# Ternary weights of the first block: ScalarE writes the group scale, VectorE decides by a bf16 difference and makes the first weights' low parts, with new turns and PSUM places for the whole program

## The reference

```python
def ternary_quant(w_fp32, g=64):
    w = w_fp32.astype(jnp.bfloat16)
    w_g = w.reshape(-1, g)
    scale = jnp.clip(jnp.mean(jnp.abs(w_g), axis=-1, keepdims=True), 1e-08, None)
    q = jnp.clip(jnp.round(w_g / scale), -1, 1)
    return w + stop_gradient((q * scale).reshape(w.shape) - w)

gate, up = jnp.split(x @ ternary_quant(w_gate_up).T, 2, axis=-1)
h = jax.nn.silu(gate) * up
out = rms_norm(h) @ ternary_quant(w_proj).T

xn = layernorm(x)                       # block 0, attention
q, k, v = xn @ Wq + bq, xn @ Wk + bk, xn @ Wv + bv
```

## Time and profile before

| | |
|---|---|
| median of 3 runs | 1232.33 us |
| span of the profiled execution | 1229.5 us |
| the profiled execution's own time | not given beside its span; the median of the runs lies 2.8 us above the span |
| PE busy | 1096.5 us, 89% of the span |
| DVE busy | 864.2 us, 70% |
| ACT busy | 631.2 us, 51% |
| POOL busy | 503.0 us, 41% |

### The profile page before, as it was taken

How to read it: one execution, slowest core, us unless ns; L and a number is a source line. 1 busy time by engine, 2 the same in 40 slices (tenths; PEclk the granted TensorE clock), 3 DMA queues, 4 the chain that set the end, 5 groups by cost and what they waited for, 6 DMA issues and landing times.

```text
span 1229.5 us, 17428 instructions
## 1 busy us (share of the span) xinstructions
PE 1096.5 (89%) x6541; PEld 718.4 (58%) x6556; DVE 864.2 (70%) x1612; ACT 631.2 (51%) x963; POOL 503.0 (41%) x551
## 2 busy tenths in 40 slices
PE   4579999999999998999389999998789998996998
PEld 2356686765665564675268898987234543553445
DVE  6988767678658999856667326368776779668751
ACT  4445656475568875643235224252176276455473
POOL 5655748466514544413764214053331321141131
PEclk9769999999999999999689999999699999998999
DMA  5905335443260000267350000008626316317220
GB/s 178 291 10 156 81 96 161 126 123 107 49 207 35 35 35 9 82 206 243 94 52 26 1 1 1 1 26 201 156 51 155 108 45 165 92 49 173 71 72 18
DMA packets 86115, 116.42 MB, mean 95 GB/s; under 512 B 29616, under 2 KB 43280, under 8 KB 85264
## 3 DMA queue, kind: packets, MB, share of 16 engines
q1 hardware_dynamic: 47792, 70.28, 19.1%
q0 software_dynamic: 38240, 45.03, 14.7%
HBM read 81.54 MB, written 40.40 MB: 99 GB/s over the span
## 4 chain that ended last, share of the span: by engine, by line
PE 64%; DVE 21%; ACT 5%; issue 4%; POOL 3%; DMA 2%; another core or an unknown queue 0%; SPq 0%; ACTq 0%; DVEq 0%; POOLq 0%
PE pair L691 22%; PE bank L691 19%; PE bank L770 7%; PE pair L760 5%; PE pair L749 5%; DVE max L1152 4%; ACT probs L1670 2%; POOL gathered L2082 1%; PE pair L710 1%; PE bank L778 1%; DVE hidden L1208 1%; DVE hidden L1206 1%; DVE tern_mask L1049 1%; PE pair L790 1%; DVE mix_h L1540 1%
## 5 line engine op out<-in xcount | busy, mean ns | idle before, releaser
L1152 DVE TENSOR_REDUCE max<-pair 128x2 f32<-128x1024 f32 (+3 forms) x256 | 252.6, 1020 | 64.1 <-PE pair L749 36.6
L1670 ACT ACTIVATE probs<-pair 128x1024 f32<-128x1024 f32 (+3 forms) x256 | 213.4, 865 | 112.9 <-PE pair L760 106.4
L749 PE MATMUL pair<-ks,qs 64*128 64x512 f32 (+3 forms) x512 | 111.7, 457 | 28.7 <-DVE max L1152 13.9
L770 PE MATMUL bank<-probs,v 128*32 128x512 f32 (+3 forms) x1024 | 119.0, 542 | 2.0 <-ACT probs L1670 1.3
L760 PE MATMUL pair<-qs,ks 64*128 64x512 f32 (+3 forms) x512 | 103.8, 437 | 13.7 <-DVE max L1152 4.9
L2003 POOL TENSOR_TENSOR h_low<-hidden,h_high 128x512 fp32r<-128x512 f32 x64 | 83.3, 1307 | 77.4 <-ACT h_high L1708 77.0
L749 PEld LDWEIGHTS pair<-ks,qs 64*128 64x128 f32 x512 | 50.8, 198 | 89.2 <-DVE max L1152 35.1
L760 PEld LDWEIGHTS pair<-qs,ks 64*128 64x128 f32 x512 | 46.5, 190 | 81.2 <-ACT probs L1670 25.9
L2100 POOL TENSOR_TENSOR h<-mix_h,h 128x512 bf16<-128x512 f32 x48 | 54.8, 1169 | 75.4 <-DMA h<-comb 49.7
L1702 ACT ACTIVATE hidden<-pair 128x512 f32<-128x512 f32 x64 | 38.0, 597 | 86.5 <-PE pair L691 72.6
L2047 POOL TENSOR_SCALAR_AFFINE_SELECT probs<-probs 128x256 f32<-128x256 f32 x128 | 51.3, 411 | 65.0 <-ACT probs L1670 63.8
(11 more groups left out here) (327 smaller groups left out, 2678.5 us busy)
## 6 DMA issues: line engine op xcount, KB each, us to landing
kept<-q_high SPq DMA_DIRECT2D x64, 256.0 KB, 3.7
qs<-kept POOLq DMA_DIRECT2D x32, 512.0 KB, 4.2
ks<-kept POOLq DMA_DIRECT2D x32, 512.0 KB, 5.2
kept<-q_low SPq DMA_DIRECT2D x32, 256.0 KB, 4.1
expert_in<-in_experts_in SPq DMA_DIRECT2D x16, 352.0 KB, 4.3
expert_out<-in_experts_out SPq DMA_DIRECT2D x16, 256.0 KB, 5.5
h<-comb SPq DMA_DIRECT2D x4, 1024.0 KB, 5.4
x<-in_x SPq DMA_DIRECT2D x4, 512.0 KB, 5.1
```

Of the source, the lines that this page charges most:

```text
L749: made = mm(to[:, hh, 0:n], m.qs[k][slot][r0:r0 + STACK, p, qt * P:(qt + 1) * P], m.ks[k][slot][r0:r0 + STACK, p, 0:n], start=True, stop=k ...
L770: made = mm(to[32 * j:32 * j + 32, q0:T], m.v[b % 2][:, kt, G * g + j, :], m.probs[(2 * kt + j // 2) % 4][:, j % 2, q0:T], start=kt == 0, ...
L1152: V.tensor_reduce(m.max[:, g % 2, :, p, qt], to[:, :, 0:n], AX.X, ALU.max).then_inc(*s.done("top"))
L1670: A.activation(m.probs[(2 * kt + p) % 4][:, :, q0:T], to[:, :, q0:T], ACT.Exp, scale=0.25).then_inc(*s.done("exp"))
```

## The change

- `tern_mean(j)`, a new part on ScalarE, reads the sum from PSUM and writes the scale as bf16. It frees the PSUM place, which `tern_scaled` freed before.
- `tern_scaled(j)` has four instructions in place of five, and none reads PSUM: scale minus magnitude (with the lower bound of 1e-8), the comparison of that difference with the magnitude, magnitude plus difference, and the product.
- `split_first` on VectorE makes the low parts of block 0's Wq, Wk and Wv. `split_low(0)` on GpSimd goes.
- `headed` waits for the `headed` two places earlier, on its own engine.
- Turns (DUE) of all engines and PSUM places (TAKEN) are new.

```diff
@@ DUE (one line of some 150)
-    "tern_sum": "0 2 3 4 7 9 8 10 17 15 16 26",
+    "tern_sum": "0 1 3 4 6 9 8 10 17 13 16 27",
...
@@ FREED
-    "tern_sum": lambda j: [("tern_scaled", (j,))],
+    "tern_sum": lambda j: [("tern_mean", (j,))],
@@ qk and vals, TensorE
-        pe.wait_ge(*at("split_low", k // 3))
+        pe.wait_ge(*(at("split_low", 1) if k else at("split_first")))
@@ VectorE
+    def split_first():
+        dve.wait_ge(*at("split_high", 0))
+        V.tensor_tensor(m.wqk_low[0][:, :, :], m.wqk[0][:, :, :], m.wqk_high[0][:, :, :].bitcast(F32), ALU.subtract).then_inc(*dve.up())
+        V.tensor_tensor(m.wv_low[0][:, :, :], m.wv[0][:, :, :], m.wv_high[0][:, :, :].bitcast(F32), ALU.subtract).then_inc(*s.done("split_first"))
     def tern_scaled(j):
-        t, to = m.tern[j % 3], bank("tern_sum", j)
-        dve.wait_ge(*at("tern_sum", j))
-        V.tensor_scalar(t["scale"][:, :], to[:, 0, :], 1.0 / 64, 1e-8, ALU.mult, ALU.max).then_inc(*dve.up())
+        t = m.tern[j % 3]
+        dve.wait_ge(*at("tern_mean", j))
+        V.scalar_tensor_tensor(t["scale"][:, :], t["scale"][:, :], 1e-8, t["mag"][:, :], ALU.max, ALU.subtract).then_inc(*dve.up())
         dve.wait_ge(*dve.own())
         if j >= 3:
             dve.wait_ge(*at("tern_out", j - 3))
-        V.scalar_tensor_tensor(t["mask"][:, :], t["scale"][:, :], 257.0 / 512, t["mag"][:, :], ALU.mult, ALU.is_lt).then_inc(*dve.up())
-        dve.wait_ge(*dve.own())
-        V.tensor_tensor(t["mask"][:, :], t["mask"][:, :], t["scale"][:, :], ALU.mult).then_inc(*dve.up())
-        dve.wait_ge(*dve.own())
-        V.tensor_tensor(t["scale"][:, :], t["mask"][:, :], t["mag"][:, :], ALU.subtract).then_inc(*dve.up())
-        dve.wait_ge(*dve.own())
-        V.tensor_tensor(t["mask"][:, :], t["mag"][:, :], t["scale"][:, :], ALU.add).then_inc(*s.done("tern_scaled"))
+        V.tensor_tensor(t["mask"][:, :], t["scale"][:, :], t["mag"][:, :], ALU.is_lt).then_inc(*dve.up())
+        V.tensor_tensor(t["scale"][:, :], t["mag"][:, :], t["scale"][:, :], ALU.add).then_inc(*dve.up())
+        dve.wait_ge(*dve.own())
+        V.tensor_tensor(t["mask"][:, :], t["mask"][:, :], t["scale"][:, :], ALU.mult).then_inc(*s.done("tern_scaled"))
@@ headed, VectorE
+        if 4 * b + g >= 2:
+            dve.wait_ge(*at("headed", k, *((b, g - 2) if g >= 2 else (b - 1, g + 2))))
@@ ScalarE
+    def tern_mean(j):
+        act.wait_ge(*at("tern_sum", j))
+        A.activation(m.tern[j % 3]["scale"][:, :], bank("tern_sum", j)[:, 0, :], ACT.Abs, scale=1.0 / 64).then_inc(*s.done("tern_mean"))
```

More of the change, by code:

```diff
@@ L70 @@
     "DVE": {
-        "set_dve": [(0,)], "tern_scaled": keys(range(12)),
+        "set_dve": [(0,)], "split_first": [()], "tern_scaled": keys(range(12)),
         "stat": keys(ALL, B, range(TT)), "cut_low": keys((0, 2, 3), B),
@@ L86 @@
     "ACT": {
-        "tern_cast": keys(range(12)), "norm": keys(ALL, B, range(TT)), "turned": keys(ALL, B),
+        "tern_cast": keys(range(12)), "tern_mean": keys(range(12)), "norm": keys(ALL, B, range(TT)), "turned": keys(ALL, B),
         "biased": keys(B, PAIRS), "q_high": keys(HEADS, B, PAIRS), "exp": keys(HEADS, B, range(G), range(TT), PAIRS), "summed": keys(HEADS, B, range(G)),
@@ L98 @@
     "POOL": {
-        "cast0": [()], "split_low": keys(range(3)), "bring": keys(HEADS, B, range(G)), "max_bring": keys(HEADS, B, range(G)), "tern_out": keys(range(12)),
+        "cast0": [()], "split_low": keys((1, 2)), "bring": keys(HEADS, B, range(G)), "max_bring": keys(HEADS, B, range(G)), "tern_out": keys(range(12)),
         "root": keys(ALL, B), "based": keys(HEADS, B), "with_xn": keys(B),
@@ L326 @@
-    "weigh": "77776666666666666666666677776666666677777777777766666666666666667777666666666666777766667777666677776666777777777777777777776666",
-    "back": "77677667666677777776767676766677",
-    "rows": "402004020442",
-    "out": "76677767666776767676766776667667",
-    "unit": "2402020420004202220202044042044220422040024204202044200424402044",
-    "down": "77767677",
-    "mean": "6777",
-    "proj": "0044022402200440",
-    "gate": "7766667776676776",
-    "gamma": "4024",
-    "inflow_turn": "0202",
@@ new lines @@
+    "weigh": "77776666666666666666777777777777666677776666777766667777666666667777666666666666666666667777777777776666777777777777666666667777",
+    "back": "67666676676677767776766676767667",
+    "rows": "442004044420",
+    "out": "67767767776776767666676776666676",
+    "unit": "2402020420004202400242044002244204422040040240242204424044422244",
+    "down": "77766677",
+    "mean": "7766",
+    "proj": "0444020402200440",
+    "gate": "6667667776776776",
+    "gamma": "4024",
+    "inflow_turn": "2202",
@@ new lines @@
+    "mem_turn": "77776666",
+    "shared": "0202440220420442",
+    "count": "7666",
+    "logit_turn": "7776",
+    "merge": "67",
+    "expert_turn": "6767776777766677",
+    "expert_in": "4224242042400224",
+    "expert_fold": "7767766666766766",
+    "expert_out": "6667766677777667",
+    "spline": "204024022040",
+    "qk2": "2440",
+    "v2": "76766776",
+    "score2": "6776677677767676",
+    "probs_turn": "7676677767667776",
+    "comb_turn": "6766",
+    "mix": "402402020240040402024220200402424220422402004220",
@@ L1540, in mixed @@
         V.scalar_tensor_tensor(h, m.mix_t[j % 2][:, :], 1.0, to[:, 1, :], ALU.add, ALU.mult).then_inc(*s.done("mixed"))
-    parts = {"set_dve": set_dve, "tern_scaled": tern_scaled, "half": half, "stat": stat, "cut_low": cut_low, "v_out": v_out,
+    parts = {"set_dve": set_dve, "split_first": split_first, "tern_scaled": tern_scaled, "half": half, "stat": stat, "cut_low": cut_low, "v_out": v_out,
              "rope": rope, "q_low": q_low, "top": top, "shift": shift, "headed": headed, "joined": joined, "fed": fed, "gated": gated,
@@ L1926, in mix_tanh @@
         A.activation(m.mix_t[j % 2][:, :], to[:, 0, :], ACT.Tanh, scale=0.5).then_inc(*s.done("mix_tanh"))
[L1928 removed]
+    parts = {"tern_cast": tern_cast, "tern_mean": tern_mean, "norm": norm, "turned": turned, "split_high": split_high, "biased": biased, "q_high": q_high, "exp": exp, "summed": summed, "rowed": rowed, "tanh": tanh, "high": high, "square": square,
              "proj_out": proj_out, "convd": convd, "gate_sig": gate_sig, "gamma_out": gamma_out, "qk_square": qk_square, "norm_root": norm_root, "mem_out": mem_out,
```

34 lines of the change are left out of this document (8 added, 26 removed), and 280 rows, old and new, of the table DUE.

## The result

Four runs of the changed kernel gave a median of 1215.2 us (1210.44 to 1225.31), 0.988 of the kernel before (95% interval 0.983 to 0.993). Two more sets gave 0.992 (0.989 to 0.995) and 0.988 (0.985 to 0.991); the mean over all 16 runs, each against the kernel before on its chip, is 0.9895, or 12.9 us of 1230; from the scatter of the 16 runs this mean is good to some 0.002, 2.4 us. The forecast was 1228.2 us, 4.1 less than before, with 1222 as its lower end. All experiments are read against that 0.9895.

The account below looks back on a forecast made before the run. VectorE was taken to bound the first 92 us, TensorE what follows. Start terms -1.4 - 2.5 - 0.2 = -4.1 us, all else 0, gave 1232.3 - 4.1 = 1228.2 us; range 1222 to 1234.

Parts of the forecast that it names:

- The start: Up to the first maximum: -1.4 us to `cut_low`, -2.5 to 42.98 us, -0.2 for tiles 9, 8, 10; together -4.1 us.
- hold-ups: VectorE's ternary tiles: waiting inside instructions while GpSimd reads SBUF; 8.9 us before, about 13 us forecast.
- my first rival: VectorE's start: hold-ups stay at 8.9 us, so VectorE saves 6.2 us, up to 8.2 with turns; 1225 us, chance 0.15.
- Given back: Rival: start gains, but a later stage hanging on loads, gathers or the new order takes it back; 1232 us, chance 0.18.
- my second rival: The rival that later loads, gathers or order take back the start's gain: 1232 us, between 1230 and 1234, chance 0.18.
- ScalarE ahead of `xn`: Start: two scales and the split precede `xn`, moving it to 13.3 us, `cut_high` 2.9 us later; VectorE gets there no earlier.
- Turns from 92 us on: New order behind the start: neighbour swaps before 369 us worth at most 7 us idle; all taken as 0, 2 us either way.
- At the gathers: GpSimd before block 2: one `spline_low` of 1.28 us leaves the chain but waits 1.6 us for a spline product; net +0.3.
- `tern_mean` on ScalarE at 0: ScalarE: 12 x 0.60 = 7.2 us of added scales cost 0, or 1.2 us if each cost its hand-over.
- PSUM places ...: 0: PSUM places and the wait in `headed`, for a part long done on its own engine: 0.
- Hold-ups carried to all tiles: Rival: VectorE's tiles all wait for GpSimd's previous `tern_out`, 20.4 us of waiting; +5.3, 1237.6 us, chance 0.13.
- The lock: VectorE instructions with two SBUF inputs and GpSimd instructions reading SBUF exclude each other; without it 3.4 us more gain.

Follow-up runs that it names:

- experiment 2: Start and later turns exchanged apart: new code and turns up to 100 us with the old kernel's turns behind gave 1224.46 us, 0.996; the converse 1222.31 us, 0.994.
- start_old: The kernel before, code and turns, up to about 100 us, with the changed kernel's turns and PSUM places from there on: 1222.31 us, 0.994.
- Experiment 4: Changed kernel with the scale read by VectorE again (1236.84 us), or with the first weights' split back on GpSimd (1225.14 us, again 1220.09 us).
- scale_dve: Changed kernel with the scale read from PSUM by VectorE again, place freed by `tern_scaled`, tiles 8 and 10 exchanged, tile 11 one maximum earlier: 1236.84 us, 1.005.
- experiment 3: The edits with the order and PSUM places of the kernel before, new parts put in where they can first run: 1231.06 us, 1.002.

## Why the prediction was wrong

- **The start** (-4.1): right as an end effect, 5.0 us (2.8 to 7.1) in experiment 2, but by two misses that cancel, which is luck. `cut_low` ended at 20.15 (19.7 forecast), tile 7 at 37.33 (39), the first maximum began at 56.36 (58 to 61), the TensorE piece at 65.06 (69). So the start had gained 8.0 there. VectorE's tiles and split took 31.9 + 2.9 = 34.8 us in place of 40.7, 5.9 less, since the hold-ups were 9.1 us and not 13: my first rival's condition held. The other 2 us I haven't traced. Tiles 4, 6 and 7 had none, as the sum said; tile 3 lost 1.74 us, tile 2 0.84 and tile 5 0.82, 3.4 where I took 4.6; of the four tiles behind, two lost 3.0 and 2.0 and two nothing, where I took 5.5 for three and left tile 11 open to 2.7. The plain comparison took 0.425, as taken.
- **Given back**: 3.7 us at 98 us, by transfers that SyncE's new order had put ahead of the maxima. This is my second rival's mechanism, in a stage that I had called 97% busy and safe. I had noted the moved load and not asked what lands beside it. The rival's time (1230 to 1234) was not met, since other turns gained.
- **ScalarE ahead of `xn`**: `xn` ran from 13.69 to 15.76 (13.3 to 15.4 forecast). `cut_low` did wait for ScalarE, by 0.54.
- **The failed step: "Turns from 92 us on. ... I take 0 for all, with 2 us either way."** In its place the runs show 7.1 us faster for these turns together (4.1 to 10.3, start_old), and by stretch +7.6 (slower), -6.3 and -11 to -13 us (faster). I had argued from the share of TensorE (97% up to 369 us), and for that stretch alone there was a reason; for the rest there was none. Behind 850 us TensorE had gaps that my rows did not contain: 333.81 busy of 379.5 us before, 46 us idle, at a mean clock of 0.94. A table of turns that is new throughout can win or lose there as much as at the start.
- **At the gathers** (+0.3): the wait for the spline's product was real and larger, 4.5 us; alone it is not to be seen in the time.
- **`tern_mean` on ScalarE at 0**: nothing speaks against the 0 for its own 7 us in the new order, but it also frees the PSUM place early, which I had dismissed ("PSUM places ...: 0"). Experiment 4 shows that the new order and places can't do without that: 3.9 us at the first product, and 18 us with all that scale_dve changes; experiment 3 shows the converse, that without the order it gains nothing.
- **Hold-ups carried to all tiles** (slower, 1237.6): out, 9.1 us with the split's, against the 15.1 needed. The lock holds for pairs that meet; how many meet is the order's to say.

## What to carry to other kernels

When a change redraws the whole order, price each stage by its own idle time and not by the stage that the change names; the largest gain here lay 800 us behind the edits. Exchange the order piece by piece at points where both have done the same work: here this and the move of three loads found 11 us that the change was losing. And for a transfer of a few KB that an engine waits for, look at what large loads the queue puts beside it.
